# The places of four edge tiles by one register load, and without the bounds' check

## The reference, cut to what matters

```python
def _rgcn_layer(x, W, self_w, b, src, dst, edge_type, num_nodes):
    xW = jnp.einsum('ni,rio->rno', x, W)
    msg = xW[edge_type, src]
    agg = jax.ops.segment_sum(msg, dst, num_segments=num_nodes)
    return agg + x @ self_w + b
...
x = x + _L0_gnn_ref(_layernorm(x, axis=-1), ..., edge_index, edge_type_8)
x = x + _L0_ffn_ref(_layernorm(x, axis=-1)[None], ...)[0]
x = x + _L1_gnn_ref(_layernorm(x, axis=-1), edge_index, ...)
x = x + _L1_ffn_ref(_layernorm(x, axis=-1)[None], ...)[0]
```

## Time and profile before

| | |
|---|---|
| three runs | 2229.14 us median (2226.66 to 2229.56) |
| the profiled execution's own time | 2224.04 us |
| its span, first to last instruction | 2222.3 us |
| busy over the span | PE 1832.0 us, DVE 1424.8, POOL 895.0, ACT 885.2 |
| mean granted TensorE clock | 0.913 of full |
| DMA | 464.55 MB |

### The profile page before, as it was taken

The page is one execution under the profiler, slowest core; times in us unless marked ns, Lnnn a source line. Parts: engine busy times, 40 slices in busy tenths (PEclk is TensorE's granted clock), DMA queues, the critical chain, the costliest instruction groups (busy, mean ns, idle before and its releaser), DMA issues. The chain is left out here.

```text
span 2222.3 us, 41295 instructions
## 1 busy us (share of the span) xinstructions
PE 1832.0 (82%) x12484; PEld 1518.9 (68%) x12484; DVE 1424.8 (64%) x3320; ACT 885.2 (40%) x2059; POOL 895.0 (40%) x859
## 2 busy tenths in 40 slices
PE   2688888886788888873799999499898955999987
PEld 1467766664667666763688888378687944888866
DVE  6677777774777777654466666555454756777755
ACT  2554555534444444420133333255454520333332
POOL 1677767643776666730143343210000001333432
PEclk9999999997999999986799999699999955999988
DMA  4799998976888888876636242447676576224261
GB/s 155 256 314 300 308 296 300 308 264 216 295 289 288 267 283 275 287 249 237 250 72 216 47 119 35 127 167 253 204 251 230 177 263 264 59 42 126 40 213 20
DMA packets 200081, 464.55 MB, mean 209 GB/s; under 512 B 25476, under 2 KB 101232, under 8 KB 195728
## 3 DMA queue, kind: packets, MB, share of 16 engines
q1 hardware_dynamic: 139144, 311.14, 38.8%
q0 software_dynamic: 58112, 147.77, 24.9%
q10 hardware_dynamic: 2568, 2.56, 0.4%
HBM read 297.80 MB, written 116.39 MB: 186 GB/s over the span
## 5 line engine op out<-in xcount | busy, mean ns | idle before, releaser
L1491 PE MATMUL ps<-fixed,sums 128*128 128x256 f32 x1280 | 393.7, 422 | 57.4 <-DVE sums L1351 56.1
L1346 DVE TENSOR_TENSOR sums<-sums,ps 128x256 f32 x626 | 263.4, 421 | 263.7 <-PE ps L1462 146.1
L1173 POOL DMA_INDIRECT rows<-tab_h,gidx_node x313 | 313.7, 1002 | 175.5 <-issue 81.9
L1462 PE MATMUL ps<-slots,rows 128*128 128x128 bf16 x3756 | 322.1, 227 | 67.7 <-DMA rows<-tab_x,gidx_node 29.7
L1173 POOL DMA_INDIRECT rows<-tab_x,gidx_node x313 | 311.3, 995 | 163.0 <-issue 83.9
L1462 PEld LDWEIGHTS ps<-slots,rows 128*128 128x128 bf16 x3756 | 269.7, 102 | 144.6 <-issue 68.4
L2289 PE MATMUL ps<-ring,halves 128*128 x1128 | 289.7, 406 | 14.5 <-SPq L2251 10.8
L2405 ACT ACTIVATE x_all<-ps 128x512 f32<-128x512 f32 x188 | 113.4, 603 | 464.8 <-PE ps L2308 464.8
L2320 PE MATMUL ps<-ring,halves 128*128 x752 | 282.6, 410 | 4.0 <-DVE halves L2361 4.0
L1491 PEld LDWEIGHTS ps<-fixed,sums 128*128 128x128 f32 x1280 | 227.0, 204 | 78.5 <-DVE sums L1351 61.7
L1950 PE MATMUL ps<-node_rows,blocks 128*128 128x512 f32 (+1 forms) x1200 | 256.0, 364 | 0.6 <-ACT blocks L1832 0.6
(11 more groups left out here) (260 smaller groups left out, 2689.7 us busy)
## 6 DMA issues: line engine op xcount, KB each, us to landing
ring<-split_weights SPq DMA_DIRECT2D x16, 4096.0 KB, 14.6
sums<-fixed SPq DMA_DIRECT2D x80, 576.0 KB, 6.3
split_weights<-fixed SPq DMA_DIRECT2D x176, 256.0 KB
slots<-tab_counts SPq DMA_DIRECT2D x40, 640.0 KB, 4.2
fixed<-in_ffn_units SPq DMA_DIRECT2D x88, 256.0 KB
split_weights<-weight_pieces SPq DMA_DIRECT2D x80, 256.0 KB, 2.6
tab_counts<-fixed SPq DMA_DIRECT2D x20, 640.0 KB, 5.8
strip<-tab_counts SPq DMA_DIRECT2D x20, 640.0 KB, 4.2
```

The source lines that it names most:

```text
L1173: nc.gpsimd.indirect_dma_start(rows[:, s * PARTS * D:(s + 1) * PARTS * D], None, table, bass.IndirectOffsetOnAxis(ap=gidx[:, t:t + 1], axi ...
L1346: v.tensor_tensor(to, to, psS[t % len(psS)][:, 0:KD * P].rearrange("p (s w) -> p s w", w=WIN), ALU.add).then_inc(added, 1)
L1462: last = t_.matmul(psS[t % len(psS)][:, k * P:(k + 1) * P], rows[:, at:at + P], hots[:, h * P:(h + 1) * P], start=(n == 0), stop=(n == PAR ...
L1491: last = t_.matmul(to, lhs, weights[:, at:at + D], start=(n == 0), stop=(n == PRODUCTS - 1))
```

## The change

`add` no longer reads its place. A new helper `places_of(g)` reads the places of a group of four tiles (the last group has one) by one register load into four registers, and leaves out the run-time check of their bounds. It is called once in four steps, ahead of the first `add` of the group; each `add` is given its register. The waits, the adds themselves and all other work stay as they are.

```diff
-                def add(t):
-                    at = dve.value_load(self.at[0:1, t:t + 1], min_val=0, max_val=(SUMS - 1) * SUMW + P - 1)
+                def places_of(g):
+                    tiles = slice(g * GROUP, min((g + 1) * GROUP, ETILES))
+                    _, values = nc.values_load_multi_w_load_instructions(
+                        self.at[0:1, tiles], engines=[mybir.EngineType.DVE], min_val=0, max_val=(SUMS - 1) * SUMW + P - 1,
+                        skip_runtime_bounds_check_because="edge_layout clamps each tile's first node to its drift")
+                    return values
+
+                def add(t, at):
...
                 for t in range(steps):
                     if t < ETILES:
-                        add(t)
+                        if t % GROUP == 0:
+                            first_nodes = places_of(t // GROUP)
+                        add(t, first_nodes[t % GROUP])
```

## The result

The changed kernel took **2148.28 us** (median of 4 runs, 2146.66 to 2151.08) against 2228.52 us for the kernel before on the same chip: ratio 0.9642, 95% interval 0.9625 to 0.9659, so 80 us or 3.6% faster. A second measurement, with its own runs of before beside it, gave 2149.6 us and 0.9658 (0.9643 to 0.9673). The forecast was 2174; what came is the first rival, 2148, inside the range.

The account below looks back on a forecast made before the run. DVE's sequencer was taken to bound the later stretches, making PE and the gather ring wait. 40.3 us of ring idle plus 14.4 us of lag gave 55 us off the 2229 us median: 2174 us, range 2145 to 2207.

Parts of the forecast that it names:

- the first rival: Relational layers: only DVE's lateness held PE, so the gathers' pace is reached in full; 2148 us, chance 0.15.
- What bounds the kernel before: Later stretches of both layers: DVE's sequencer, at 0.8 us a quick tile, makes PE and the ring wait.
- The two bounds: Most the layers could gain: 82.6 us read from the gathers, 80.3 us from PE's waits for DVE.
- The load of four: DVE's 158 loads of four places: 0.4 us each taken, with 0.31 and 1.24 us as ends.
- the second rival: Each place in a load costs its own trip, so half the gain stays, 28 us: 2201 us, chance 0.20.
- the fourth: Slower: the four-place load itself stalls, deciding at 3.2 us a load; 2292 us, chance 0.04.
- The share that was taken: Part of the layers' possible gain expected: 40.3 us of ring idle plus 14.4 us of lag, 55 us.
- the ring's idle: POOL's gathers held by a full ring in the later stretches: 17.0 and 36.7 us, three quarters expected to go.
- the lag's fall: Last add's delay behind last gather, from 23.1 and 23.6 us to 9.3 and 8.5; half taken, 14.4 us.
- The signs to look for: Values expected in the new profile for loads, DVE idle, PE and ring waits, gather pace, lag, DMA and layer ends.
- Add 13 to 18 us behind: Expected delay of each layer's last add behind its last gather in the new profile: 13 to 18 us.
- The third: No change: PE's waits for DVE become waits for ACT or transfers, DMA being full; 2229 us, chance 0.06.

Follow-up runs that it names:

- e1: The kernel before with only the register work and bounds check behind each single-place load left out: 2166.68 us, ratio 0.972.
- e2: The kernel before with four places read by one load but all four checks kept: 2175.36 us, ratio 0.9761.
- e11: The changed kernel with a load, register work and check put back, unused, ahead of every second add: 2172.96 us, ratio 0.9764.
- e4: The kernel before with the load, its register work and its check done twice for every tile: 2593.7 us, ratio 1.1638.
- e5: The changed kernel with one gather in four left out, every fourth tile using the previous tile's rows: 2078.28 us, ratio 0.9332.
- e7: The kernel before without the DMAs that clear the sums, semaphores kept: 2153.09 us.
- e3: The kernel before with no register loads for the places, each tile added at a constant expected place: 2137.95 us, ratio 0.9596.

## Why the prediction was right in its direction and short in its size

**What bounds the kernel before: right.** DVE's sequencer, by its register loads and checks, made PE and the ring late. e1, e2 and e11 move the time by that line alone, and e4 shows the queue was full.

**The two bounds: right in kind, a little high.** They stood at 82.6 us by the gathers and 80.3 by PE's waits for DVE, both read from the trace of the kernel before. Against that trace the new one is 75.6 us shorter. Term by term: the gathers of layer 0 take 8.4 us less from first to last (bound 17.0) and those of layer 1 36.3 (bound 36.7); the lag of the last add fell by 16.7 and 14.9 us (bound 13.8 and 15.1), in layer 0 even below the 9.3 us that was taken as the floor.

**The load of four: right.** Forecast 0.4 us, measured 0.354 at the median, though 0.57 on the mean. The Trainium skill's 200 ns per register (Runtime: NRT & Kernel Launch, Instruction fetch mechanics) does not hold for this load: four registers took 337 ns in the quickest case and eight 593. The page tells it of loads from HBM, and these places lie in SBUF, the core's own memory. With it falls the second rival, and the fourth, which needed a load of 3.2 us. But "a fixed trip with little for the word" holds only up to four: the next four places cost 256 ns more.

**The share that was taken: wrong.** "I take three quarters of the ring's idle, 12.8 + 27.5 = 40.3 us, and half of the lag's fall, 6.9 + 7.5 = 14.4 us." The ring's part was nearly met in sum, 44.7 us (8.4 in layer 0, less than the 12.8 taken, and 36.3 in layer 1, more than the 27.5). The mis-sized term is the lag's: 14.4 us were taken and 31.6 came. Of the 25 us that the forecast fell short, 17 are the lag, 4 the ring, and 5 are no gain in any trace: the forecast took the gain from a profiled execution that was 5.1 us under its median and set it against the median, and the changed kernel's profiled execution (2148.5) was at its own median (2148.28).

The reason given for taking only a share was that PE would be 91% and 94% busy and DMA at 0.95 and 0.97; why that should cost half of the lag's fall, no row said. It came to 89% in both stretches (265.3 of 298, 254.9 of 285) and 0.93 and 0.95, and neither was late enough to matter: the gathered rows came late only by short waits, and the pace was POOL's own step (e5, e7). In layer 1 PE's work in the stretch also shrank, from 269.4 to 254.9 us, at a granted clock of 0.99 in place of 0.91. In layer 0 it did not (263.1 and 265.3 us, 0.95 and 0.99). So PE's work was not quite the fixed load it was read as, but that explains at most a part.

**The signs to look for.** Idle by "issue" under 30 us: 10.7. Waits for merge and one-hots under 25: 9.8 in both layers. POOL's wait for the ring down to a few us: 6.1 and 3.4. Gathers once in 1.31 to 1.38 us: 1.32 and 1.30. DMA at 0.92 or more: yes, in the later stretches. Add 13 to 18 us behind: it is 6.4 and 8.7, the one sign that spoke for the first rival, and the term that was mis-sized. The layers end 24.5 and 51.1 us shorter, where 20 and 35 were given.

**The rivals.** The first (0.15) is what happened: DVE's lateness was all that held PE. That its 2148 was hit to less than 1 us is in part luck: its 81 us stand against 75.6 in the traces, and the other 5 come from the quick profiled execution of the kernel before. The third, no change because transfers eat the gain, fell: PE does wait for gathered rows now, 104 us in both layers against 50, but only because it is early.

## What to carry to other kernels

An engine that is busy 72% can still be the bound: count what its sequencer does per step (register loads, checks, waits), which no busy share shows, and hold that against the step's time. When two independent readings of the waits agree on a bound, as 82.6 and 80.3 us did here (75.6 came in the trace), take most of it unless a row gives a reason for less; the half taken of the lag had none of its own and was the largest error. Once a queue has left the path, stop: removing the last loads moved the layers by some 2 us at most (e3), and a quarter of the gathers that stand behind was worth 70 us. And look for the odd one in a group before reading its minimum: here the quickest load of each batched form was the one that had a single place.

## What the runs showed of the hardware that was not expected

- PE's granted clock in the later stretches was higher where PE was busier: 0.83 over the layers where the doubled line left it 70% busy, 0.95 and 0.91 before at 86% and 84%, 0.99 with the change at 89%, 0.99 and 1.00 without a quarter of the gathers at 96% and 90%. The busy share alone does not order it: in the first stretch of layer 0 (61 to 178 us) the two traces of the change have 1.00 at 77% and 0.96 at 80%, the two of eight places 0.88 at 80% and 0.96 at 79%. That gaps lower the clock was not tried by itself.
- A register load of one word takes 297 ns in the quickest case, of four words 337 and of eight 593. The medians of the whole rows are 309, 354 and 790 ns.
- In the relational layers 31% of single-word loads took over 0.5 us and up to 1.76; in the experts' stages of the same kernel none did. Without the DMAs that clear the sums it was 18%, with small loads of weight pieces still 30%; the rest is open.
